# Causal mask of a score bank: one 128-row product in the place of four 32-row products

## The reference

```python
scores = jnp.einsum('bhqd,bhkd->bhqk', Qh, Kh)
scores = (scores + jnp.einsum('bhqd,qkd->bhqk', Qh, rel_k)) / scale
causal = jnp.tril(jnp.ones((S, S), dtype=bool))
scores = jnp.where(causal[None, None], scores, -1e9)
attn = jax.nn.softmax(scores, axis=-1)
```

## Time and profile before

| what | value |
|---|---|
| median of 3 runs | 1033.54 us (1032.39 to 1035.63) |
| profiled execution, its own time | 1030.79 us |
| its span, first to last instruction | 1029.1 us |
| mean granted clock of TensorE over the span | 0.939 |
| TensorE busy, products | 898.8 us (87%), 8935 products |
| VectorE busy | 817.6 us (79%) |
| ScalarE busy | 680.5 us (66%) |
| GpSimd busy | 728.0 us (71%) |

### The profile page before, as it was taken

One profiled execution on the slowest core, in us unless ns is written; L12 is line 12 of the kernel. 1 busy time (PEld: TensorE's weight loads), 2 busy tenths in 40 slices (PEclk: granted clock), 3 DMA queues, 4 the chain that ended last, 5 costly groups with the idle time before them and its releaser, 6 DMA issues. The chain is left out here.

```text
span 1029.1 us, 25739 instructions
## 1 busy us (share of the span) xinstructions
PE 898.8 (87%) x8935; PEld 526.4 (51%) x8935; DVE 817.6 (79%) x1948; ACT 680.5 (66%) x1315; POOL 728.0 (71%) x946
## 2 busy tenths in 40 slices
PE   2888988999899988998999898887679999999995
PEld 0443444544445444444444444433357777777773
DVE  4787888888888888887888888876667888878884
ACT  3247777767668777776777867665346767676773
POOL 5244686686776867768668777566257989898886
PEclk9999999989889999898899998987889999999998
DMA  3311111111111111111111111001425454545541
GB/s 82 137 34 26 29 43 28 35 46 27 29 27 38 43 28 33 40 27 35 28 36 46 28 31 37 25 26 43 162 62 156 150 170 153 164 150 166 163 138 31
DMA packets 58828, 70.88 MB, mean 69 GB/s; under 512 B 8944, under 2 KB 34416, under 8 KB 58720
## 3 DMA queue, kind: packets, MB, share of 16 engines
q1 hardware_dynamic: 56432, 69.04, 23.1%
q10 hardware_dynamic: 2288, 0.42, 0.2%
HBM read 43.75 MB, written 8.65 MB: 51 GB/s over the span
## 5 line engine op out<-in xcount | busy, mean ns | idle before, releaser
L1137 DVE TENSOR_REDUCE mx<-ps_s 128x1 f32<-128x512 f32 (+2 forms) x640 | 410.2, 682 | 75.2 <-PE ps_s L1549 74.2
L809 ACT ACTIVATE prob<-ps_e 128x512 f32<-128x512 f32 x640 | 352.0, 608 | 110.3 <-PE ps_e L1506 110.2
L651 POOL TENSOR_SCALAR_AFFINE_SELECT prob<-prob 128x516 f32<-128x516 f32 (+1 forms) x320 | 176.6, 576 | 150.2 <-ACT prob L809 150.1
L1530 PE MATMUL ps_s<-ks,qs 31*128 31x512 f16 (+3 forms) x1024 | 196.5, 324 | 32.2 <-DVE mx L1137 27.0
L1572 PE MATMUL ps_av<-prob,vp 128*32 128x512 f32 (+3 forms) x2048 | 202.5, 495 | 4.3 <-POOL prob L651 4.2
L731 POOL TENSOR_TENSOR hidden_low<-hidden,hidden_high 128x512 fp32r<-128x512 f32 x144 | 191.0, 1354 | 12.0 <-ACT hidden_high L998 10.7
L1506 PE MATMUL ps_e<-qs,ks 32*128 32x512 f16 (+3 forms) x1024 | 167.9, 316 | 6.2 <-ACT prob L809 2.0
L1530 PEld LDWEIGHTS ps_s<-ks,qs 31*128 31x128 f16 x1024 | 54.9, 94 | 167.6 <-issue 89.4
L1549 PE MATMUL ps_s<-masked_at,below 32*128 32x64 bf16 (+3 forms) x2560 | 135.0, 192 | 0.0
L998 ACT CAST hidden_high<-hidden 128x512 fp32r<-128x512 f32 x160 | 98.0, 613 | 30.7 <-DVE hidden L1450 27.5
L1549 PEld LDWEIGHTS ps_s<-masked_at,below 32*128 32x128 bf16 x2560 | 105.6, 98 | 20.0 <-issue 4.1
(11 more groups left out here) (173 smaller groups left out, 1664.3 us busy)
## 6 DMA issues: line engine op xcount, KB each, us to landing
gate_rows<-gates_dram SPq DMA_DIRECT2D x128, 256.0 KB, 3.7
qs<-qh SPq DMA_DIRECT2D x64, 64.0 KB, 2.1
xnT_dram<-oT SPq DMA_DIRECT2D x16, 256.0 KB, 2.0
xeT<-xnT_dram SPq DMA_DIRECT2D x16, 256.0 KB, 2.8
out<-result SPq DMA_DIRECT2D x16, 256.0 KB, 2.3
v_near<-v_back SPq DMA_DIRECT2D x16, 254.0 KB
ks<-kh SPq DMA_DIRECT2D x62, 64.0 KB, 2.1
qs<-ql SPq DMA_DIRECT2D x32, 64.0 KB, 2.1
```

Of the source, the lines that this page charges most:

```text
L651: pool.affine_select(out=v, in_=v, compare_op=ALU.is_ge, fill=0.0, base=-2, pattern=cols, channel_multiplier=-1).then_inc(S["p_masked"], 1)
L809: act.activation(prob[g % 2][:, u, b, :], ps_e[bank][:, :], ACT.Exp, scale=SCALE).then_inc(S["e_done"], 1)
L1137: dve.tensor_reduce(out, src, AX.X, ALU.max).then_inc(s_free[bank], 1)
L1530: pe.matmul(scores[:, at:at + P * (qt + 1)], qs[par][rows, pr, P * qt:P * qt + P], ks[par][rows, pr, 0:P * (qt + 1)], start=(n == 0), stop ...
```

## The change

Each bank is masked by one product over all 128 rows: `below` whole as the weights, and as moving columns either 129 or 257 neighbouring columns of `masked_at`, now 257 wide (one or two diagonal patterns behind each other), or for u = 2 twice 129 columns, since there the two diagonal blocks are apart. The order in the round is unchanged. The copies on ScalarE and their semaphore go, and GpSimd's eight selects become four.

```diff
-        below = [sb(f"below{i}", [P, P], BF16) for i in range(4)]
-        masked_at = sb("masked_at", [P, QUAD + 1], BF16)
+        below = sb("below", [P, P], BF16)
+        masked_at = sb("masked_at", [P, 2 * P + 1], BF16)
...
-                for i in range(8):
-                    columns = slice(0, QUAD) if i < 4 else slice(QUAD, QUAD + 1)
-                    v = masked_at[:, columns]
-                    pool.affine_select(out=v, in_=v, compare_op=ALU.not_equal, fill=MASKED,
-                                       base=-QUAD * (i % 4) - (0 if i < 4 else M_ROW),
-                                       pattern=[[-1 if i < 4 else 0, v.shape[1]]],
+                for i, (base, lo, hi) in enumerate(((0, 0, P), (1 - P, P, P + 1), (-1, P + 1, 2 * P), (1 - P, 2 * P, 2 * P + 1))):
+                    v = masked_at[:, lo:hi]
+                    pool.affine_select(out=v, in_=v, compare_op=ALU.not_equal, fill=MASKED, base=base,
+                                       pattern=[[-1 if hi - lo > 1 else 0, hi - lo]],
                                        channel_multiplier=1).then_inc(S["masked_made"], 1)
...
-            def roll_quads():
-
-                act.wait_ge(S["const_ready"], N_POOL_CONST)
-                for turn in range(1, 4):
-                    for c in range(4):
-                        src = QUAD * ((c + turn) % 4)
-                        act.copy(below[turn][QUAD * c:QUAD * c + QUAD, :],
-                                 below[0][src:src + QUAD, :]).then_inc(S["rolled"], 1)
...
-            def diagonals(bank, u, part):
...
-            def s_mask(g, u, bank, part, b):
...
-            def s_masks(g, u, both):
-
-                for part in range(4):
-                    for b in (1, 0):
-                        s_mask(g, u, both[b], part, b)
+            def s_masks(u, both):
 
                 n = len(S_UNITS[u])
+                for b in (1, 0):
+                    if u == 2:
+                        blocks = both[b].rearrange("p (n c) -> p n c", n=n)[:, :, P - 1:2 * P]
+                        columns = masked_at[:, 0:P + 1].unsqueeze(1).to_broadcast([P, n, P + 1])
+                    else:
+                        blocks, columns = both[b][:, SEQ - n * P - 1:SEQ], masked_at[:, 0:n * P + 1]
+                    pe.matmul(blocks, below[:, :], columns, start=False, stop=True).then_inc(S["s_full"], 1)
...
                     pe.wait_ge(S["const_ready"], N_CONST)
-                    pe.wait_ge(S["rolled"], 12)
-                    pe.wait_ge(S["masked_made"], 8)
+                    pe.wait_ge(S["masked_made"], 4)
```

More of the change, by code:

```diff
@@ L392, in block_kernel @@
         names = """
-            attn_loaded qk_loaded x_loaded0 x_loaded1 x_loaded2 const_made const_ready rolled bias_full bias_ready
+            attn_loaded qk_loaded x_loaded0 x_loaded1 x_loaded2 const_made const_ready bias_full bias_ready
             m_made masked_made v_rows k_rows q_rows
@@ L575, in _ @@
             zeros(pool.memset(ident16[:, :], 0.0))
-            zeros(pool.memset(below[0][:, :], 1.0))
+            zeros(pool.memset(below[:, :], 1.0))
             zeros(pool.memset(masked_at[:, :], 0.0))
@@ L589, in _ @@
                                    pattern=[[-1, P]], channel_multiplier=1).then_inc(S["const_ready"], 1)
-            pool.affine_select(out=below[0][:, :], in_=below[0][:, :], compare_op=ALU.is_ge, fill=0.0, base=0,
+            pool.affine_select(out=below[:, :], in_=below[:, :], compare_op=ALU.is_ge, fill=0.0, base=0,
                                pattern=[[-1, P]], channel_multiplier=1).then_inc(S["const_ready"], 1)
@@ L985, in step @@
                     first_keys()
-                    roll_quads()
             def end_out(f, s):
@@ L1797, in step @@
                     if st.A:
-                        s_masks(S_GROUP[g], u, both)
+                        s_masks(u, both)
                     for kt in {1: (0,), 2: (1, 2,), 4: (3,)}.get(u, ()):
```

## The result

Five runs of the changed kernel have a median of 1042.15 us (1040.65 to 1043.06), five of the kernel before 1035.5 (1032.39 to 1035.63): a ratio of 1.0072, 95% interval 1.0054 to 1.0089. It is slower by 6.65 us, inside the range of 1024 to 1080; the forecast was +16. The profiled execution of after took 1042.29 us, its span is 1040.6; that of before took 1030.79, less than any of the five, so the profiles differ by 11.5 us where the medians differ by 6.65. What follows is about the profiles.

The account below looks back on a forecast made before the run. No engine is full in the attention part; TensorE has the least room and ends most waits. 33 us passed on - 15 clock - 2 start = +16 on 1030.8, 1046.8; median 1049 us, forecast's own range 1035 to 1072, overall 1024 to 1080.

Parts of the forecast that it names:

- The block: Mask products in 320 rounds on TensorE: 54 us longer at full clock, 3.4 us a step, 44 of it in two-block rounds.
- round 15: One-block round followed by scores: masks to next scores 0.55 us against 0.30, +0.25, 16 rounds, 4 us.
- The 0.11 us: Pause on TensorE that each change of tile size costs, ahead of the masks and, before another tile, behind them.
- the load at nothing: Mask weight loads cost nothing, hidden behind the product before; the uncovered first might add up to 98 ns, 31 us in all.
- Rival 4: Count of small products is what is paid, so fewer make it faster: -15 - 2, about 1017 us; chance 0.06.
- How much passes: Share of TensorE's added 54 us that reaches the end: 0.6, 33 us, between 18 and 48.
- rival 3: TensorE's idle time takes up the whole addition (3.4 of 3.7 us a step), only the start left: 1031 us; chance 0.12.
- The clock: TensorE's granted clock, 0.93 over 104 to 650 us, loses 38 us; the change gives 15 back.
- Rival 2: The clock stays up and returns its 38 us, deciding beyond 34: -7, 1027 us for the median; chance 0.14.
- The reason given: Clock: longer mask blocks fill waits for maxima, perhaps the short ones, and put 128-row work into rounds of mostly 32-row products.
- The start: First scores of step 1 come earlier without the 12 ScalarE copies: 2 us gained, 2.9 at best, 0 at least.
- the signs that the prediction named: Among them: VectorE's and ScalarE's waits for TensorE grow, TensorE's for maxima shrink; wrong if those keep their length.

Follow-up runs that it names:

- the one-column product: Kernel before with one zero product of 128 rows and one column ahead of each round's eight 32-row masks: 1082.48 us, 1.0458 of before.
- two-block kernel: Kernel before with 128-row masks only in the two-block rounds (u = 1, 2, 4), the start as before: 1047.49 us, 1.0124 of before.
- one-block rounds only: Kernel before with 128-row masks only in the one-block rounds (u = 0, 3), the start as before: 1026.78 us, 0.9918 of before.
- column tiles: Changed kernel with two-block rounds' masks cut into four products of 128 rows by 32 columns of weights: 1024.63 us, 0.9899 of before.
- masks twice: Changed kernel with each 128-row mask product issued twice: 1056.5 us, 1.0195 of before.
- 256 zero columns: Kernel before with a zero product of 128 rows and 256 columns ahead of each round's 32-row masks: 1095.06 us, 1.06 of before.

## Why the prediction was right, and where its sizes were off

**The block: right but for round 15.** Predicted 54 us of TensorE, measured about 45: two-block rounds +0.20 us (192, 39 us; predicted +0.23), one-block rounds ahead of 128 x 128 products +0.03 (64 of the 80, 2 us), rounds 0 and 3 about +0.12 (32, 4 us), rounds 15 and 18 nothing. For round 15 the prediction worked out 0.30 us before and +0.25; the trace of before has 0.60, since the next scores wait for a maximum, and that wait hides the longer block; in round 18 a wait for ScalarE does the same. The 0.11 us is shown by the one-column product, the load at nothing by the two-block round: 0.32 us from the first mask to the value products are 2 x 0.115 for the columns and 0.09 of pause. The Trainium skill (TensorEngine Tiling (Array Packing), section Tiling Modes) has the drain at a change of mode and none between tiles of one mode; the traces agree, with 0.11 us and, from mask to projection, nothing. Rival 4, the count of products, is refuted by the two-block kernel: with fewer products it is slower.

**How much passes: the mis-sized term.** The prediction had 0.6 of the whole, 33 us. At equal clock it is 1.21 us of 45 / 16 = 2.8 a step, 0.43, or 19 us. Steps at 0.96 from all kernels show why (us; before and after are the means above, the one-block and two-block kernels the means of nine and seven steps, the others the rows shown, from which their other steps at 0.96 differ by at most 0.3):

```
kernel                   step   TensorE busy   idle
before                  40.89      36.26       4.6
one-block rounds only   40.86      36.61       4.3
column tiles            40.98      37.09       3.9
after                   42.10      38.83       3.3
two-block rounds only   42.07      38.42       3.6
one zero column         42.85      39.69       3.2
masks twice             43.69      41.55       2.1
256 zero columns        44.20      41.52       2.7
```

Up to column tiles, 0.83 us more of busy TensorE costs 0.09: idle time takes it, as rival 3 has it. From there to masks twice, 4.46 more cost 2.71, 0.61 of it. So the fraction taken was that of the further time, and the first part has cover. At equal clock the two-block rounds alone cost what the whole change costs, and the one-block rounds nothing. That the cover is the idle time is read from these rows; which waits give it up was not isolated, and steps of one kernel differ by up to 1.1 us.

**The clock: right in sign, smaller.** Predicted -15 of 38 us. It rose from 0.93 to 0.96, 16 us of TensorE at the lower level; the steps got back 19 - 12.1 = 7 us in the profiles, or 0.74 x 16 = 12 by the steady steps. Rival 2 wanted more than 34. The reason given was in part wrong: long waits stayed, and the clock no longer fell behind one.

**The start: -1.7 of -2 in the profile, not shown by runs.** So 19 - 7 - 1.7 + 1.1 = 11.4 of the span's 11.5, against the +16 forecast; it closes because the 7 is what the steps leave over. With the steady steps' 12 the sum is 6.4, and the medians differ by 6.65.

Steady steps are the better guide to the runs. Sixteen times the difference between their mean, at whatever clock they ran, and before's 41.63 gives +7.5 us for after (runs +6.65), +12 for the two-block kernel (+12.7), -11 for the one-block kernel (-8.0) and -10 for column tiles (-10.4); of the kernels here only the one with 256 zero columns is off by more than 4 us (+53 against +60). So most of the 5 us by which the two profiles differ more than the medians lies outside the steady steps, in the first four and behind the last, and need not be the change's.

Of the signs that the prediction named, two did not come. TensorE's waits for maxima shrank by 2.7 of 27.0 us only, and the longest kept its 1.4 us, which it had counted as a sign of being wrong; ScalarE's waits did not grow.

**Still open:** why the granted clock rose (the runs show in which kernels, and that a longer block is not enough), why 256 zero columns cost 12.6 us more than one, and whether the start reaches the end of the kernel.

## What to carry to other kernels

Give a small product the tile size of a neighbour, not the fewest instructions: with 128 x 32 masks ahead of the 128 x 32 value products the kernel is 1.0% faster than before, where 128 x 128 ones in their place make it 0.7% slower. Most of that 1.0% is the one-block rounds' gain (0.8% alone): the old 32-row masks, which share the tile size of the scores ahead of them, do nearly as well in the two-block rounds, and the runs do not tell the two apart. Split a change by the kinds of place that it touches before judging it: here one kind gained 8 us and the other lost 13. Compare steps at equal granted clock first, then ask what the change does to the clock.

## What the runs showed of the hardware

The granted clock of 104 to 650 us went from 0.93 to 0.96 with 128-row masks, 0.97 with each issued twice, and down to 0.89 with one-column products ahead of the 32-row ones; a step of before at 0.88 took 2.8 us longer than one at 0.96. Four products of 128 x 32 side by side take the time of one: two banks of 257 columns in 0.23 us, the same as two whole-array products. And the clock column can read 1.00 ahead of the first change that was recorded, where durations say half speed.
